# Splitting the relative-shift round trip of an attention phase into half transfers on the SyncE queue

## The reference, cut to what matters

```
q, k, val = heads(x @ Wq + bq), heads(x @ Wk + bk), heads(x @ Wv + bv)
pos       = heads(sinusoid @ Wp + bp)                       # 512 x 16 for each head
content   = einsum('bhsp,bhtp->bhst', q + u, k)             # 512 x 512 for each batch and head
position  = _relative_shift(einsum('bhsp,htp->bhst', q + v, pos))
weights   = softmax((content + position) / sqrt(16))
out       = einsum('bhst,bhtp->bhsp', weights, val) @ Wo + bo

def _relative_shift(x):                                     # x: b, h, s, s
    x = pad(x, one zero in front of every row)              # rows of s + 1
    x = x.reshape(b, h, s + 1, s)                           # the same bytes, read as rows of s
    return x[:, :, 1:, :].reshape(b, h, s, s)
```

## Time and profile before

| what | value |
|---|---|
| median of 3 runs | 5177.69 us (5159.45 to 5185.83) |
| the profiled execution, its own time | 5203.23 us |
| its span | 5200.9 us |
| TensorE busy | 4993.4 us (96%) |
| VectorE busy | 3715.1 us (71%) |
| ScalarE busy | 3464.4 us (67%) |
| bytes moved by DMA | 1391.47 MB, mean 268 GB/s |
| `write_x`, `read_x` | 512 of each, median 9.6 us and 8.6 us from issue to landing |

### The profile page before, as it was taken

How to read it: one execution, slowest core, us unless ns; L and a number is a source line. 1 busy time by engine, 2 the same in 40 slices (tenths; PEclk the granted TensorE clock), 3 DMA queues, 4 the chain that set the end, 5 groups by cost and what they waited for, 6 DMA issues and landing times. The chain is left out here.

```text
span 5200.9 us, 126426 instructions
## 1 busy us (share of the span) xinstructions
PE 4993.4 (96%) x42412; PEld 3718.9 (72%) x42412; DVE 3715.1 (71%) x8040; ACT 3464.4 (67%) x5180; POOL 1431.9 (28%) x1032
## 2 busy tenths in 40 slices
PE   7899999999999999999999999997999999999997
PEld 3566666666666666666666666666999898998996
DVE  7699898887887877888878788884445555443344
ACT  3688788787887877878878778873433333344444
POOL 1111111121111111211111111103555555544443
PEclk9799999999999999999999999998999999999998
DMA  9899999999999999999999999987355455532349
GB/s 353 308 353 329 327 343 329 331 336 324 335 330 336 338 331 333 342 332 338 332 332 338 326 332 337 346 299 245 73 125 130 113 133 132 126 64 52 76 126 317
DMA packets 320378, 1391.47 MB, mean 268 GB/s; under 512 B 42816, under 2 KB 120384, under 8 KB 188352
## 3 DMA queue, kind: packets, MB, share of 16 engines
q1 hardware_dynamic: 270528, 1315.45, 74.3%
q0 software_dynamic: 49152, 67.14, 7.3%
HBM read 708.20 MB, written 674.23 MB: 266 GB/s over the span
## 5 line engine op out<-in xcount | busy, mean ns | idle before, releaser
L677 DVE CUSTOM_DVE_ANT_0 att_shifted<-att_quad,att_shifted 128x512 f32<-128x512 f32 x2048 | 1330.5, 684 | 249.4 <-PE att_quad L921 202.6
L542 ACT ACTIVATE att_shifted<-att_shifted,att_mn 128x512 f32<-128x512 f32 x2048 | 1361.0, 717 | 129.7 <-issue 129.3
L537 ACT ACTIVATE att_xo<-att_quad 128x1024 f32<-128x1024 f32 x1024 | 1048.4, 1024 | 462.9 <-PE att_quad L909 462.6
L687 DVE COPY att_pt<-att_tp 128x512 f32<-128x512 f32 x1536 | 1012.8, 686 | 214.4 <-PE att_tp L942 213.3
L942 PE MATMUL att_tp<-att_ident,att_shifted 128*128 128x128 f32 x8192 | 1153.5, 285 | 0.9 <-DVE att_pt L687 0.4
L942 PEld LDWEIGHTS att_tp<-att_ident,att_shifted 128*128 128x128 f32 x8192 | 904.5, 144 | 305.9 <-issue 283.3
L1405 DVE TENSOR_TENSOR ffn_hp<-ffn_hf,ffn_hp 128x512 fp32r<-128x512 f32 x512 | 478.2, 934 | 686.0 <-ACT ffn_hf L1343 685.2
L1341 ACT ACTIVATE ffn_hp<-ffn_up 128x512 fp32r<-128x512 f32 x512 | 306.1, 598 | 925.0 <-PE ffn_up L1486 924.8
L909 PE MATMUL att_quad<-att_pos,att_qv 64*128 64x512 f32 x2048 | 852.8, 456 | 30.3 <-ACT att_xo L537 30.2
L921 PE MATMUL att_quad<-att_kd,att_qu 64*128 64x512 f32 x2048 | 777.5, 457 | 70.8 <-issue 55.3
L1447 PE MATMUL ffn_yp<-ffn_w2p,ffn_hp 128*128 128x256 f32 x6144 | 828.9, 285 | 14.7 <-DVE ffn_ys L1374 12.4
(11 more groups left out here) (108 smaller groups left out, 4830.1 us busy)
## 6 DMA issues: line engine op xcount, KB each, us to landing
xs_d<-att_xo SPq DMA_DIRECT2D x512, 1026.0 KB, 9.6
att_shifted<-xs_d SPq DMA_DIRECT2D x512, 1024.0 KB, 8.6
att_shifted<-in_L_attn_x_dram SPq DMA_DIRECT2D x32, 512.0 KB, 7.2
xn_d<-att_shifted SPq DMA_DIRECT2D x32, 512.0 KB, 6.4
xt_d<-att_shifted SPq DMA_DIRECT2D x32, 512.0 KB, 7.4
att_xf<-xt_d SPq DMA_DIRECT2D x32, 512.0 KB, 9.2
att_d<-att_osb SPq DMA_DIRECT2D x512, 32.0 KB
ffn_d<-ffn_zero SPq DMA_DIRECT2D x8, 2048.0 KB, 24.9
```

The source lines that it names most:

```text
L537: act.activation(xo[:, kk % NW, 2 * half:2 * half + 2, 1:S + 1], xp[:, :, :], ACT.Copy).then_inc(x_out, 1)
L542: act.activation(shifted[:, kk % NX, t], shifted[:, kk % NX, t], ACT.Exp, bias=mn[:, kk % NX, t:t + 1], scale=-1.0).then_inc(exp_done, 1)
L677: dve.tensor_tensor_reduce(out=shifted[:, kk % NX, t], in0=sp_[:, t % 2], in1=shifted[:, kk % NX, t], scale=-0.25, scalar=-NEG, op0=ALU.ad ...
L687: dve.tensor_copy(pt[:, t], tp[:, t % 2]).then_inc(t_out_dve, 1)
```

## The change

`write_x` and `read_x` take a third argument, `half`, and move only the rows t = 0, 1 or t = 2, 3 of every partition, on both sides of the transfer. A transfer of 128 x 2052 numbers becomes two of 128 x 1026, and one of 128 x 2048 becomes two of 128 x 1024. Every half still adds 16 to its semaphore, so that all waits on `x_written` and `x_shifted` now count 32 for each head. Each half write waits, as before, for both halves of ScalarE's copy, and each half read for both halves of its head's write. In the body of a head the order is: first half of the write of `kk + 4`, first half of the read of `kk + 3`, second half of the write, second half of the read, and then `load_xt` and `store_o` where they were. In the prologue the two halves of each write and of each read follow one another.

```diff
--- before.py
+++ after.py
@@ -339,21 +339,25 @@
                         load_xt(0)
                 store_xt(B - 1)
 
-                def write_x(i, kk):
+                def write_x(i, kk, half):
 
                     slot, turn = of_slot(kk)
+                    part = slice(2 * half, 2 * half + 2)
                     wait_alone(sp, x_out, (i * BH + kk + 1) * 2)
 
-                    wait_alone(sp, x_shifted[slot], (i * (BH // NX) + turn) * 16)
-                    sp.dma_start(xs_d[slot].rearrange("(p t c) -> p t c", t=TT, c=S + 1), xo[:, kk % NW]).then_inc(x_written[slot], 16)
-
-                def read_x(i, kk):
+                    wait_alone(sp, x_shifted[slot], (i * (BH // NX) + turn) * 32)
+                    sp.dma_start(xs_d[slot].rearrange("(p t c) -> p t c", t=TT, c=S + 1)[:, part], xo[:, kk % NW, part]
+                                 ).then_inc(x_written[slot], 16)
+
+                def read_x(i, kk, half):
 
                     slot, turn = of_slot(kk)
-                    wait_alone(sp, x_written[slot], (i * (BH // NX) + turn + 1) * 16)
+                    part = slice(2 * half, 2 * half + 2)
+                    wait_alone(sp, x_written[slot], (i * (BH // NX) + turn + 1) * 32)
 
                     wait_alone(sp, t_full, (i * BH + kk - NX + 1) * TT)
-                    sp.dma_start(shifted[:, slot], xs_d[slot][S:S + S * S].rearrange("(p t c) -> p t c", t=TT, c=S)).then_inc(x_shifted[slot], 16)
+                    sp.dma_start(shifted[:, slot, part], xs_d[slot][S:S + S * S].rearrange("(p t c) -> p t c", t=TT, c=S)[:, part]
+                                 ).then_inc(x_shifted[slot], 16)
 
                 def store_o(i, q):
 
@@ -370,23 +374,26 @@
                 sp.wait_ge(p_low, DC)
                 sp.wait_ge(w_low, 1)
                 for k in range(LEAD - 1):
-                    write_x(0, k)
+                    write_x(0, k, 0)
+                    write_x(0, k, 1)
                     if k == 2:
                         for n in range(NS):
                             sp.wait_ge(xn_stored[n], 16 * (B // NS))
                             sp.wait_ge(xt_stored[n], 16 * (B // NS))
                     if k:
-                        read_x(0, k - 1)
+                        read_x(0, k - 1, 0)
+                        read_x(0, k - 1, 1)
                 load_xt(1)
 
                 def body(i):
                     first = isinstance(i, int) and i == 0
                     last = isinstance(i, int) and i == ITERS - 1
                     for kk in range(BH):
-                        if not (last and kk + LEAD - 1 >= BH):
-                            write_x(i, kk + LEAD - 1)
-                        if not (last and kk + LEAD - 2 >= BH):
-                            read_x(i, kk + LEAD - 2)
+                        for half in range(2):
+                            if not (last and kk + LEAD - 1 >= BH):
+                                write_x(i, kk + LEAD - 1, half)
+                            if not (last and kk + LEAD - 2 >= BH):
+                                read_x(i, kk + LEAD - 2, half)
                         if kk % H == 4 and not last:
                             load_xt(i * 2 + 2 + kk // H)
                         if kk % QH == 0 and not (first and kk < 2 * QH):
@@ -532,7 +539,7 @@
 
                     if half == 0 and not (isinstance(i, int) and i * BH + kk < NW):
                         slot, turn = of_slot(kk - NW)
-                        act.wait_ge(x_written[slot], (i * (BH // NX) + turn + 1) * 16)
+                        act.wait_ge(x_written[slot], (i * (BH // NX) + turn + 1) * 32)
                     act.wait_ge(x_full, (i * BH + kk) * 2 + half + 1)
                     act.activation(xo[:, kk % NW, 2 * half:2 * half + 2, 1:S + 1], xp[:, :, :], ACT.Copy).then_inc(x_out, 1)
 
@@ -672,7 +679,7 @@
                     n = i * BH + kk
                     if t == 0:
                         slot, turn = of_slot(kk)
-                        wait_alone(dve, x_shifted[slot], (i * (BH // NX) + turn + 1) * 16)
+                        wait_alone(dve, x_shifted[slot], (i * (BH // NX) + turn + 1) * 32)
                     wait_alone(dve, s_full, n * TT + t + 1)
                     dve.tensor_tensor_reduce(out=shifted[:, kk % NX, t], in0=sp_[:, t % 2], in1=shifted[:, kk % NX, t], scale=-0.25,
                                              scalar=-NEG, op0=ALU.add, op1=ALU.min,
```

## The result

The change makes the kernel slower: 5602.22 us (5592.97 to 5604.75, 4 runs) against 5180.11 us (5159.45 to 5185.83, 4 runs), a ratio of 1.082 with a 95% interval of 1.0799 to 1.0842. That is 422 us, where 260 were forecast. The sign is as forecast, and so is one of the two places of the loss, the one behind the stores; the other, the heads without stores, was put at nothing. The time lies 8 us inside the upper end of the range and outside the case that was held likeliest (5350 to 5530).

What follows compares the result with a forecast made beforehand. TensorE and transfers were taken as balanced, 24.5 against 25.5 us for four heads; 2.2 us more behind the stores gave 282 us, less 22 covered, so 5178 + 260 = 5438, rounded to 5440 us, range 5155 to 5610.

Steps and rivals of the forecast that it cites:

- the heads without stores: Three of every four heads, also called plain heads: each still takes 5.84 us from read to read, no loss.
- the upper end: Top of the range, 5610 us, past the point where a quarter of a microsecond comes on top of each head.
- the case that was held likeliest: The order of the transfers costs time only behind the stores, 2.2 us in four heads: 5350 to 5530 us, chance 0.47.
- The bound: In the heads, TensorE (24.5 us for four) and the transfers (25.5 us) are balanced; a slower transfer pace has no room.
- The place behind the stores: Every fourth head: the half write behind the stores finds the DMA engines dry, 2.2 us more in four heads.
- The step that failed: In heads without stores, 2.9 us queued at the landing suffice, with 0.7 to 1.1 us to spare.
- dearer: Packet ends count or the 0.7 us to spare is missing: 0.25 to 0.5 us more each head, 5570 to 5700; chance 0.15.
- The other half of that rival: In the heads' transfers, twice the packets with odd ends cost up to 0.5 us more in every head, 256 us.
- Faster: The heads' finer mix of halves moves faster, as in the normalising stage, at 383 GB/s: 5133 us, chance 0.13.
- No change: The 2.2 us gap behind the stores is covered because SyncE runs ahead after each loop stall: 5178 us, chance 0.10.
- part covered: Half the loss behind the stores is covered by TensorE's stall at the turn of the loop: 5300 us, chance 0.12.
- The rival built on it: The fixed cost shows in every head, three more gaps of 1.8 us in four heads: 6130 us, chance 0.03.

Runs made afterwards that it cites:

- The two pairs of kernels: The kernel before and the change, each with its block of stores (5180.11 and 5602.22 us) and with stores spread over four heads (5135.29 and 5322.26 us).
- everything covered: Halves: the change with reads one head later and stores spread, 5114.8 us; whole transfers: the kernel before with stores spread, 5135.29 us.
- the two kernels with spread stores that were run in both: The kernel before with stores spread (5135.29, then 5130.96 us), and the change with reads one head later and stores spread (5114.8, then 5116.52 us).

## Why the prediction was right in kind and short in size

*The bound.* Right. The kernel was balanced between TensorE and the transfer pace, and the slower pace showed as VectorE's wait for the read, 321.3 us. Taking the stores out of the way won 40 us, and the same waits vanished.

*The place behind the stores.* Right in its mechanism: the half write behind them finds the queue dry. Its size can't be read from the spread stores alone, since these take away the old gap of 2.1 us as well. In the queue of the kernel after, four heads without a load between them take 28.8 us (two such groups, first half read at 1643.96 to 1701.53), and 4 x 6.35 = 25.4 of it are plain pace; 3.4 are the stores, 1.3 more than before, where 2.2 were forecast. Some of the shortage that was counted there is in the plain pace already. The two pairs of kernels give the block more, 235 us or 1.8 in four heads. This may be because with spread stores TensorE and not the queue sets the pace of the kernel before, so that part of the slower plain pace is still covered there; that was not measured, and the split between the two places is known only roughly.

*The step that failed* is "In a head without stores this is enough: 2.9 against a fixed part of 1.6 to 2.0 and the 0.2 of the queue's reaction". What has to be covered is not the fixed part of a write alone but the whole turn, from the landing through a read to the next write, and that was 3.3 us with nothing queued. 2.9 is less than that. Every head got some 0.5 us longer, 2.0 in four: the term that was put at nothing. All heads of the two queues from 400 to 3300 us say the same as the few rows: from read to read (in the kernel after, first half reads) the mean of the head with the stores went from 7.4 to 9.0 us, and of the three others from 6.3 to 6.8. With 1.3 and 2.0 the sum is 3.3 us for four heads, against the 3.1 that the phase shows and the 2.2 forecast. The runs put it in one table; extra time is the difference of the medians over 512 heads, all causes together, against a kernel whose heads are paced in part by TensorE.

| order in a body | queued, us | extra for each head, us |
|---|---|---|
| whole R, W | 0 | 2.99 |
| W half, R, W half | 1.7 | 1.98 |
| W half, R half, R half, W half | 1.7 | 2.07 |
| the change | 2.9 | 0.82 |
| whole W, half R, half R | 5.8 | 0.15 |
| W half, W half, R half, R half | 5.8 | 0.06 |
| the change, reads one later | 8.7 | 0.04 |

The time follows the second column, and not the number of transfers in the first. This had a place in the prediction as half of the rival "dearer" (the 0.7 us to spare isn't there), with 0.15, at 5570 to 5700; the measured time falls into it. That it also lies within the range owes something to luck. The plain heads lost 0.5 us each, twice what the upper end allowed for, and the place behind the stores lost less than forecast. With both terms at their worse values, 2.2 + 2.0 us in four heads, the prediction's own sum gives 5180 + 4.2 x 128 - 22, about 5700 us and past the range (an estimate).

*The other half of that rival*, the ends of the packets, is out: with all transfers halved and the queue deep the loss is 0.25 to 0.5%, and with the stores spread too the halves are no slower than whole transfers (5116.5 us against 5131.0 and 5139.7).

*The rivals.* Faster was wrong, and nothing speaks for its premise of a finer mix that moves faster: with everything covered, halves and whole transfers run at 347 and 343 GB/s, both at TensorE's pace. No change and part covered needed more lead than the landing times showed, and the runs gave no sign of more. The rule of the Trainium skill in "DMA: Bandwidth & Descriptors", section "Rules for kernel authors" (a megabyte or more for each transfer), would not by itself tell these kernels apart: half-megabyte transfers cost 0.5% in one order and 20% in another. The rival built on it had 1.8 us more in every plain head; in the kernel after it was 0.5, and 3.4 only with nothing queued. The same page of the Trainium skill gives about 2 us of fixed cost for a transfer, in the section "Anatomy of one DMA", but for the transfers that GpSimd issues; the prediction used this for transfers that SyncE issues. For these the trace had 2.0 for a write alone and 1.6 for a half-megabyte store, and the loop around a dependent read and write has 3.3 to hide.

*What the profile was to show.* Waits of 250 us and more: 321.3, or 290.0 in the stretch of the earlier trace rows. The stores 1.8 us after the first half read: 1.6 (1701.53 to 1703.13). The landing of 3.7 us behind the stores: 3.6. 308 GB/s: 298 and 295. 27.7 us for four heads: 28.8. Plain heads at 5.8: 6.3 to 6.4, and the prediction had said that over 6 would mean packets or the thin queue. The runs say which: the thin queue. The pace of TensorE between waits was to stay at 6.14 us, and of this there is no clean row: its 42412 matmuls were busy for 5210.3 us and not 4993.4, with the granted clock lower.

*The clock.* TensorE's granted clock was 0.90 to 0.91 in the heads (0.97 before), and TensorE was busy 217 us longer for the same matmuls. This is not a second cause of the loss to speak of, since from 400 to 3300 us the queue that sets the pace waited for ScalarE's copy, and through it for TensorE, only 15.6 us in all.

*Left open.* Subtracting what is queued from 3.3 us gives the order of the kernels but not their paces. Take the last two of the three plain heads between two blocks of stores, from 400 to 3300 us. Their medians are 9.28 us with the whole read first, 8.21 with the writes alone split, 8.27 with a half write first and last, and 6.48 with the change. Less 5.84 that is 3.4, 2.4, 2.4 and 0.6 us in the open, where the subtraction gives 3.3, 1.6, 1.6 and 0.4. Why more stays open was not settled.

## What to carry to other kernels

Where an engine's queue waits for one transfer before it issues the next ones, count the work that is already queued behind the awaited transfer, and compare it with the whole turn measured with an empty queue. Here cutting all megabyte transfers in two cost 0.5% or less when the queue was deep (the reads alone 1.6%), and putting half of a write behind the wait cost 8 to 20% beside the block of stores and 3% without it. A block of small stores in the same queue is part of that turn in the heads in which it falls, so spread it. A DMA share of 0.9 or more and a row of nines do not say that the engines keep their pace: from 400 to 3300 us the kernel after had 298 GB/s at a share of 0.91, and the same kernel with its reads one head later 334 GB/s at 0.92. Read GB/s and the distance from issue to issue.

## What the runs showed of the hardware that was not expected

A read issued into an empty queue with a write right behind it took 6.4 us to land, and the pair 9.0 (1709.01 to 1718.0); a write issued first with the read right behind took 5.4 and the pair 7.8. The same two megabytes, 1.2 us apart by their order. It is no single case: 32 such pairs with the read first, from 1000 to 1300 us of the run with the whole read first, took 8.9 us or more and 9.1 in the median, and four pairs with the write first, issued when the one before had landed (592 to 813 us in the kernel before with spread stores), took 7.7 to 8.1. And the kernel before took 5176 to 5180 us in the earlier comparisons and 5245 in the last, while the two kernels with spread stores that were run in both took 5135 and 5131, and 5115 and 5117: the balanced kernel showed a difference that the covered ones did not.
